# A transformer layer on 8 cores: the output projection moved into the attention loop, one query tile at a time

## The reference

```
x = x + attention(layernorm(x)) @ Wo
x = x + ffn(layernorm(x))
```

## Time and profile before

| what | value |
|---|---|
| median of 2 runs | 2536.53 us (2533.41 to 2539.64) |
| profiled execution, own time | 2543.05 us |
| its span on the slowest core (6) | 2541.5 us |
| spans of the 8 cores | 2519.2 to 2541.5 us |
| attention, from the first matmul to the end of the last copy into `OT` | 655.2 to 1048.9 us |
| output projection with normalization | 1049.8 to 1195.1 us |
| router tiles | 1196 to 1290 us |
| busy PE, DVE, ACT over the span | 68%, 24%, 21% |
| mean granted clock of core 6 | 0.766 |

### The profile page before, as it was taken

The page is one execution under the profiler, slowest core; times in us unless marked ns, Lnnn a source line. Parts: engine busy times, 40 slices in busy tenths (PEclk is TensorE's granted clock), DMA queues, the critical chain, the costliest instruction groups (busy, mean ns, idle before and its releaser), DMA issues.

```text
span 2541.5 us, 31073 instructions; the slowest of 8 cores (2519.2 to 2541.5 us)
## 1 busy us (share of the span) xinstructions
PE 1740.8 (68%) x8936; PEld 882.1 (35%) x8936; DVE 601.6 (24%) x1144; ACT 540.0 (21%) x1129; POOL 162.5 (6%) x290
## 2 busy tenths in 40 slices
PE   0666666555452266645747889999997999999800
PEld 0444444322231123312533334444443444444400
DVE  3332332222444455354020000000100000000055
ACT  1222224322443355211431111111110000000200
POOL 0111111000000000000000000000000000000023
PEclk9655566767555555676658999999998999999855
DMA  9322321210400000142005644444444354345134
GB/s 227 94 95 67 100 67 29 72 34 0 76 2 2 6 10 1 59 124 83 1 1 104 129 93 80 77 75 75 76 77 89 83 107 101 83 95 112 75 90 142
DMA packets 46779, 185.02 MB, mean 73 GB/s; under 512 B 6560, under 2 KB 10912, under 8 KB 37152
## 3 DMA queue, kind: packets, MB, share of 16 engines
q0 software_dynamic: 27744, 86.02, 20.2%
q1 hardware_dynamic: 18880, 97.00, 12.0%
HBM read 243.86 MB, written 25.17 MB: 106 GB/s over the span
## 4 chain that ended last, share of the span: by engine, by line
PE 59%; issue 11%; DVE 10%; ACT 9%; DMA 7%; POOL 1%; another core or an unknown queue 1%; DVEq 1%; ACTq 0%; SPq 0%; POOLq 0%
PE PSA L1119 18%; PE PSA L1084 17%; ACT arena L456 3%; PE PSA L449 3%; PE PSA L1060 3%; PE PSA L540 3%; PE PSA L695 3%; DMA arena<-xq 2%; PE PSA L567 2%; DMA arena<-we 2%; PE PSA L898 2%; PE PSA L933 2%; DVE arena L801 2%; PE PSA L982 2%; PE PSA L774 1%
## 5 line engine op out<-in xcount | busy, mean ns | idle before, releaser
L1119 PE MATMUL PSA<-arena 128*128 128x512 bf16 x2048 | 445.0, 381 | 16.6 <-DMA arena<-wd 16.6
L1084 PE MATMUL PSA<-arena 128*128 128x512 bf16 x2048 | 445.2, 380 | 8.6 <-DMA arena<-wu 8.4
L1119 PEld LDWEIGHTS PSA<-arena 128*128 128x128 bf16 x2048 | 201.0, 98 | 260.6 <-issue 20.9
L1084 PEld LDWEIGHTS PSA<-arena 128*128 128x128 bf16 x2048 | 200.6, 98 | 253.2 <-issue 14.6
L449 PE MATMUL PSA<-identb,arena 128*128 128x128 bf16 x960 | 120.9, 279 | 168.8 <-DVE arena L679 55.8
L456 ACT CAST arena<-PSA 128x512 bf16<-128x512 f32 x256 | 150.1, 586 | 194.3 <-PE PSA L449 179.9
L1093 DVE TENSOR_TENSOR arena<-arena 128x1024 bf16<-128x1024 bf16 x64 | 44.3, 692 | 577.9 <-ACT arena L1089 577.9
L449 PEld LDWEIGHTS PSA<-identb,arena 128*128 128x128 bf16 x960 | 77.1, 119 | 208.8 <-issue 203.2
L1089 ACT ACTIVATE arena<-PSA 128x1024 bf16<-128x1024 f32 x64 | 65.5, 1024 | 388.3 <-PE PSA L1084 388.3
L540 PE MATMUL PSA<-arena 128*128 128x256 bf16 x512 | 110.8, 406 | 43.9 <-DMA arena<-wk 26.9
L1060 PE MATMUL PSA<-arena 128*128 128x512 bf16 x512 | 116.5, 389 | 22.6 <-DMA arena<-we 22.4
(11 more groups left out here) (127 smaller groups left out, 1477.5 us busy)
## 6 DMA issues: line engine op xcount, KB each, us to landing
arena<-xb SPq DMA_DIRECT2D x16, 2048.0 KB, 10.3
arena<-wu POOLq DMA_DIRECT2D x64, 512.0 KB, 5.1
arena<-wd POOLq DMA_DIRECT2D x32, 1024.0 KB, 12.9
arena<-xq SPq DMA_DIRECT2D x4, 2048.0 KB, 9.6
arena<-xq SPq DMA_DIRECT2D x8, 1024.0 KB, 8.9
x1sp<-arena SPq DMA_DIRECT2D x8, 1024.0 KB, 6.1
arena<-we POOLq DMA_DIRECT2D x16, 512.0 KB, 7.0
moesp<-arena SPq DMA_DIRECT2D x16, 512.0 KB, 7.4
```

The lines of the kernel that those rows point to most:

```text
L1084: items = [(lambda e, k=k, seg=seg, sl=sl, pb=pb: e.matmul(pv(512 * pb, 512), wub[sl].rearrange("p (k c) -> p k c", k=KD)[:, k, :], xn2Tv[ ...
L1119: items.append(lambda e, kp=kp, wsl=wsl, seg=seg, pb=pb: e.matmul(pv(512 * pb, 512), wdb[wsl].rearrange("p (k c) -> p k c", k=32)[:, kp % ...
```

## The change

1. The loop of the output projection becomes a function `wo_block(j)`. It is called inside the attention loop, right behind `st3b` of tile j's last task. The barrier between attention and projection is gone. The three tasks that follow (of tile j+1) are in flight at that point.
2. The four segments of a block all use bank 6 (before: banks 0 and 1), the bank into which the transposes of attention also go.
3. The normalized tile is written over the residual buffer `xqt` instead of `xn2f`. The lost rest is written to a small buffer `xlot`, and SP stores it to memory (`xlosp`). In the router each tile's rest is loaded back by SP before that tile's transposes. The load of tile t+1 is written behind tile t's transposes of `xn2lo` and waits for them, since all tiles carry the one name `xn2lo`.
4. `reduce_sum` of a narrow task moves from `st2` to `st3a`, one step later.
5. The copy of the transposed probabilities of a narrow task takes 64 partitions instead of 128. Buffers move to other places in the arena.

```diff
@@ st2, narrow task
                         bias=stat[:, 2 + hp:3 + hp], scale=-1.0),
                       reads=[f'negS{hp}', f'st_negmax{hp}'], writes=[f'Pb{hp}'])
-                    E('vector', lambda e, hp=hp, w=w: e.reduce_sum(
-                        stat[:, 90 + 2 * hp:92 + 2 * hp],
-                        Pb[hp][:, 0:2 * w].rearrange("p (h k) -> p h k", h=2),
-                        axis=mybir.AxisListType.X),
-                      reads=[f'Pb{hp}'], writes=[f'st_rowsum{hp}'])
@@ st3a, narrow task
                 if nh == 2:
+                    E('vector', lambda e, hp=hp, w=w: e.reduce_sum(
+                        stat[:, 90 + 2 * hp:92 + 2 * hp],
+                        Pb[hp][:, 0:2 * w].rearrange("p (h k) -> p h k", h=2),
+                        axis=mybir.AxisListType.X),
+                      reads=[f'Pb{hp}'], writes=[f'st_rowsum{hp}'])
...
-                    E('scalar', lambda e, pq=pq: e.copy(
-                        out=PTs[pq][:, 0:256], in_=pv(6 * 512, 256)),
+                    E('scalar', lambda e, pq=pq, w=w: e.copy(
+                        out=PTs[pq][0:w, 0:256], in_=pv(6 * 512, 256, 0, w)),
@@ the projection
+            def wo_block(j):
+                tt = j
+                sl = tt % 2
+                E('sync', lambda e, tt=tt, sl=sl: e.dma_start(
+                    out=xqt[sl], in_=IN['xq'][128 * tt:128 * (tt + 1)]),
+                  dma=True, slot=f'xq{sl}', writes=[f'xqt{sl}'])
+                for seg in range(4):
+                    items = [(lambda e, k=k, seg=seg, tt=tt: e.matmul(
+                        pv(6 * 512, 512), OTv[:, k, 128 * tt:128 * (tt + 1)],
+                        wov[:, k, 512 * seg:512 * (seg + 1)],
+                        start=(k == 0), stop=(k == 7))) for k in range(8)]
+                    MMG(items, ['OT', 'wob'], ['bank6'])
+                    E('vector', lambda e, seg=seg, sl=sl: e.scalar_tensor_tensor(
...
+                      reads=['bank6', f'xqt{sl}'], writes=[f'x1t{sl}'])
...
+                emit_ln(x1t[sl], xqt[sl], [f'x1t{sl}'], f'xqt{sl}', par=sl)
+                E('scalar', lambda e, tt=tt, sl=sl: e.copy(out=xn2v[:, tt, :], in_=xqt[sl]),
+                  reads=[f'xqt{sl}'], writes=['xn2'])
+                E('vector', lambda e, tt=tt, sl=sl: e.tensor_tensor(
+                    out=xlot[sl], in0=xqt[sl], in1=xn2v[:, tt, :], op=ALU.subtract),
+                  reads=[f'xqt{sl}', 'xn2'], writes=[f'xlot{sl}'])
+                xlo_evs[tt] = E('sync', lambda e, tt=tt, sl=sl: e.dma_start(
+                    out=xlosp[tt], in_=xlot[sl]),
+                  reads=[f'xlot{sl}'], dma=True, slot=f'xlo{sl}')
...
                 if 0 <= step - 3 < NTASK:
                     st3b(step - 3)
+                    if step - 3 in wo_after:
+                        wo_block(wo_after[step - 3])
...
-            pr.barrier()
...
-            for tt in range(NQT):
...
@@ router, per tile
                 sl = tt % 2
+                E('sync', lambda e, tt=tt: e.dma_start(out=xn2lov[:, tt, :], in_=xlosp[tt]),
+                  extra=[xlo_evs[tt]], dma=True, slot=f'xlo{tt % 2}', writes=['xn2lo'])
```

More of the change, by code:

```diff
@@ L257, in build_program @@
     x1sp = nc.dram_tensor("x1sp", [TQ, D], F32, kind="Internal").ap()
+    xlosp = nc.dram_tensor("xlosp", [NQT, 128, D], BF16, kind="Internal").ap()
     moesp = nc.dram_tensor("moesp", [KD, 128, TQ], F32, kind="Internal").ap()
@@ L273, in build_program @@
              'mr0', 'mr1', 'wd0', 'wd1', 'wd2', 'wd3', 'gam', 'bet', 'x1r0', 'x1r1',
-             'out0', 'out1', 'xch2']
+             'out0', 'out1', 'xch2', 'xlo0', 'xlo1']
     pr = Prog(nc, slots=SLOTS)
@@ L322, in build_program @@
         Pb = [av(20 * K + i * 3 * K, KEYSP, BF16) for i in range(2)]
-        PTs = [av(26 * K + i * 3 * K, KEYSP, BF16) for i in range(2)] + [av(98 * K, KEYSP, BF16)]
+        PTs = [av(26 * K + i * 3 * K, KEYSP, BF16) for i in range(2)] + [av(106 * K, KEYSP, BF16)]
         diagb = [av(32 * K + i * 512, 128, BF16) for i in range(4)]
@@ L327, in build_program @@
         xqt = [av(82 * K + i * 8 * K, 2048, F32) for i in range(2)]
-        x1t = [av(98 * K + i * 8 * K, 2048, F32) for i in range(2)]
+        x1t = [av(176 * K + i * 8 * K, 2048, F32) for i in range(2)]
+        xlot = [av(98 * K + i * 4 * K, 2048, BF16) for i in range(2)]
         xn2 = av(144 * K, NQT * 2048, BF16)
-        xn2f = [av(116 * K + i * 8 * K, 2048, F32) for i in range(2)]
+        xn2f = [av(64 * K + i * 8 * K, 2048, F32) for i in range(2)]
         xn2lo = av(0, NQT * 2048, BF16)
@@ L907, in st3b @@
                       reads=['bank7'], writes=['OT'])
+            wov = wob.rearrange("p (k c) -> p k c", k=8)
+            xn2v = xn2.rearrange("p (t d) -> p t d", t=NQT)
+            xn2lov = xn2lo.rearrange("p (t d) -> p t d", t=NQT)
+            x1evs = []
+            xlo_evs = {}
+            def wo_block(j):
[11 more added lines that the diff above has]
+                    E('vector', lambda e, seg=seg, sl=sl: e.scalar_tensor_tensor(
+                        out=x1t[sl][:, 512 * seg:512 * (seg + 1)], in0=pv(6 * 512, 512),
+                        scalar=1.0, in1=xqt[sl][:, 512 * seg:512 * (seg + 1)],
+                        op0=ALU.mult, op1=ALU.add),
+                      reads=['bank6', f'xqt{sl}'], writes=[f'x1t{sl}'])
+                ev = E('sync', lambda e, tt=tt, sl=sl: e.dma_start(
+                    out=x1sp[128 * tt:128 * (tt + 1)], in_=x1t[sl]),
+                  reads=[f'x1t{sl}'], dma=True, slot=f'x1s{sl}')
+                x1evs.append(ev)
+                emit_ln(x1t[sl], xqt[sl], [f'x1t{sl}'], f'xqt{sl}', par=sl)
[7 more added lines that the diff above has]
+                  reads=[f'xlot{sl}'], dma=True, slot=f'xlo{sl}')
@@ L909, in build_program @@
+            last_of_j = {}
+            for i, (jx, h0x, nhx) in enumerate(tasks):
+                last_of_j[jx] = i
+            wo_after = {v: jx for jx, v in last_of_j.items()}
             for step in range(NTASK + 3):
@@ L953, in build_program @@
-            if dbg:
                 E('sync', lambda e: e.dma_start(out=DBG['d_x1'], in_=x1sp), extra=x1evs, dma=True, slot='dbg')
```

## The result

The changed kernel takes 2556.61 us (median of 11 runs), the kernel before 2535.12 (10 runs): a ratio of 1.0085 with an interval of 1.0072 to 1.0098. That is 21.5 us more, 0.85%: inside the 2% that the prediction counts as the same, and clear of no change. The profiled execution took 2552.73 us, with a span of 2551.2 on its slowest core, which is now core 0.

The account below looks back on a forecast made before the run. It took chains of waits, with no engine full, to bound narrow attention steps and projection tiles. -58 + 103 - 25 + 10 = +30 us on the profiled 2543.05 gave 2573, less 6.5 to the median: 2567, range 2530 to 2600.

Parts of the forecast that it names:

- Part 1: Narrow attention steps: moving the row sum one step later cuts 3.38 us to 1.89, 58 us less in all.
- Part 2: Projection blocks inside the attention loop: 249 us against 146 before, 103 us more if the clock stays at the lower level.
- the first three terms: Attention and projection: row sum -58, blocks +103 and the clock inside blocks -25 us.
- The clock: Matmuls inside the blocks: PE gets 0.65 instead of 0.50, 25 us less, bounds 0 and 54.
- full: Rival: blocks run at the full clock, another 29 us less, 2538 us; chance 0.17.
- lower throughout: Rival: blocks stay at the lower clock, 25 us more, 2592 us; chance 0.16.
- Part 3: Barrier before the router and its first load: sending the rest through memory costs 10 us more, bounds 6 and 25.
- Part 4: Narrow tasks' ACT copy on fewer partitions, and the moved buffers: no effect on the time.
- The rival that the narrow step would not shrink: Attention: another wait replaces the removed one; 2625 us without any gain, 2596 with half of it; chance 0.08.
- the one of late router loads: Router: loads take 11 us instead of 6.9, seven tiles lose 2 to 3 us each, 2585 us; chance 0.05.
- that a block lies beside attention: Attention loop: normalization (10.2 us) is hidden seven times and the full clock comes too, 2467 us; chance 0.03.

Follow-up runs that it names:

- the experiment: Kernel before with residuals loaded two tiles ahead and the rest sent through memory: ratio 1.0006, against 1.0001 with the early loads alone.

## Why the prediction was right

It forecast 2567 us (range 2530 to 2600), 30 above the kernel before; measured are 21.5. By its own terms:

- *Part 1, the row sum: -58.* Held: the narrow step is 1.97 us, not 1.89 (DVE's pieces take 0.08 more together), and alone the edit gives -56. That the sum's input is in time, by 0.4 us in the estimate, is shown by the missing idle time.
- *Part 2, the blocks: +103.* Held in kind and, in sum, in size: from the first scores to the end of DVE's last pass it was 539.9 us (655.2 to 1195.1) and is 560.6 (654.0 to 1214.64), 20.7 more, and the first three terms give +20. Tile 1 costs 28.3 us (DVE's last operation ends 801.29, attention resumes at 829.6), with 31.0 forecast before the clock's part of 3.1. The block of tile 0 costs 33.0 where 31.7 less 3.1 was forecast: PE was still 3 us behind with the wide transposes and products (first matmul 5.7 us behind DVE's last operation, not 2.7). Not all of that is the block's: in the kernel before, DVE waits there too, 5.82 us before the row sum at 753.45. Normalization and rest took 10.4 for 10.2.
- *The clock: -25.* The number agrees by luck. The first and the fourth addition of a block are 10.8 to 12.6 us apart, at the lower level it would be 3 x 4.76 = 14.3; over eight blocks that gives back 24.9 us on the slowest core. But it is 24.8 to 29.8 on the other cores of the same execution, and the way to the 25 was wrong twice. The average clock that I took hides two kinds of groups: in most blocks of core 0 two at 1.2 GHz (3.57 us) and then two at 2.4 (1.89 us), nearly three and one in tile 0's; on other cores there are blocks with one and with three slow ones. And the router's 0.65, which the term is made of, is no usual value. The profiled execution of the kernel before had a third level, 0.81, on six of its eight cores; on core 6 it stands in place of 1.00 in the later tiles of the projection and in most of the router. Core 2 of that execution has none of it and gets 0.73 in its router, and the changed kernel gets 0.72. First core 6 inside its router, then the whole router of core 2:

```profile
1243.50:1249.00 5.50, 3.27 (x38) 2.16 (x36) 0.00 (x0) 3.75 (x7) 0.00 (x0) 0.81 0.00 0
1192.60:1284.70 92.10, 63.85 (x640) 53.29 (x641) 0.00 (x0) 38.45 (x65) 0.00 (x0) 0.73 0.00 1
```

  With 0.73 the same working gives 3.4 x 0.50/0.73 = 2.3, so 34 us instead of 25, and a forecast of 2558. The rivals "full" and "lower throughout" are both excluded by the two kinds of groups. The rule of the Trainium skill ("TensorE: Matmul & The Clock Gate", section "Loop structure matters more than you think"), that copying out with DVE doesn't cost PE its fast clock, agrees with the trace behind the rise: gaps of 1.2 us leave PE at the full level for the rest of the block. The first groups of a block, which follow attention's steps at 0.50, are at the lower level all the same.
- With these three, 541 should have become 541 - 58 + 103 - 25 = 561, and with the longer wait for the last store it became 564.
- *Part 3, through memory: +10.* This is the mis-sized term: 7 us too much, of the 9 between forecast and result. I took 6 us for the store and 6.5 for the load from rows in which other DMAs were under way; here, with little else under way, they land in 3.2 and 3.7. The barrier is 2.2 us late, the first tile 0.6, together 3; the experiment gives 1 in an interval of 5.
- *Part 4: 0.* Not tried alone. The copy takes 0.37 us with 64 partitions as it did with 128, and the step is 1.97 us with it and 1.98 without it.

The rival that the narrow step would not shrink is excluded by the run with the sum alone; the one of late router loads by the router's 92.9 us; that a block lies beside attention by the blocks behind the loop, which cost 19 us more in all: 30.7 per tile, load wait included, against some 28 inside.

## What to carry to other kernels

Putting one stage's instructions inside another's loop overlapped nothing here, where engines take their queues in order and the inserted block is a chain between the same two engines; it hid only what another queue does, one load. Before interleaving two stages, loosen the chain inside each: asking for a result one step later gave 56 us, and a projection loop in which one pass of a tile stands behind the next tile's first additions (with early loads and four banks) some 45. A bank that every group has to share cost 36 us, more than the whole net loss. A clock read off one core of one execution can be off: compare the other cores first. And when the chain of waits charges a transfer, look what else ends at the same moment: here a load with 8.9 us on the chain was worth nothing, because a DVE chain of 10 us ended with it.

## What the runs showed of the hardware

- The granted clock rises inside a block in which PE stands still 1.2 us of every 4.8. On core 0 of the changed kernel it rose after two groups of eight 128x512 matmuls at 3.57 us each, and the next two took 1.89; on core 3 in tile 5 after one. Where the same groups stood alone between narrow steps, with 4.8 us in between (817.48 + 3.57 to the next at 825.91) and only attention's small matmuls in them, they stayed at 3.5 to 3.6.
- The profile of the kernel before shows a granted clock of 0.81 in place of 1.00: from 1150 to 1154 us on six cores, while core 2 has 1.00. The router took 93.8 us on core 6 with it (mean clock 0.65) and 92.1 on core 2 without (0.73). No run shows what brings it on.
- A store of 512 KB landed 3.2 us after its issue and a load of it in 3.7, against 7.4 and 6.5 for the same size and queue while weights were being loaded. In the changed kernel itself, with its 3.2 and 3.7, these last two are 6.9 and 7.4.
